# Quantised weights of two feed-forward layers: made in other stages, in pieces of 512 columns, and kept in DRAM as bf16

## The reference: what is computed

```python
def weight_quant(w):                     # w_gate, w_up, w_down: 2048*512 each
    scale = 1.0 / clip(mean(abs(w)), 1e-5)
    return clip(round(w * scale), -1.0, 1.0) / scale
```

```python
def absmean_quant(w):                    # w1, w2: 2048*512 each
    scale = mean(abs(w))
    mask = (abs(w) >= scale * 0.7)
    return sign(w) * mask
```

## Time and profile before

| | |
|---|---|
| median of three executions | 6014.61 us (6013.51 to 6016.92) |
| the profiled execution, its own time | 6023.15 us |
| span from its first to its last instruction | 6021.8 us |
| TensorE busy | 4680.2 us, 78% of the span |
| VectorE busy | 3349.2 us, 56% |
| POOL busy | 1794.8 us, 30% |
| ScalarE busy | 1542.7 us, 26% |
| mean granted clock of TensorE | 0.863 of full speed |

### The profile page before, as it was taken

One profiled execution on the slowest core, in us unless ns is written; L12 is line 12 of the kernel. 1 busy time (PEld: TensorE's weight loads), 2 busy tenths in 40 slices (PEclk: granted clock), 3 DMA queues, 4 the chain that ended last, 5 costly groups with the idle time before them and its releaser, 6 DMA issues. The chain is left out here.

```text
span 6021.8 us, 62767 instructions
## 1 busy us (share of the span) xinstructions
PE 4680.2 (78%) x22022; PEld 2480.6 (41%) x22022; DVE 3349.2 (56%) x5407; ACT 1542.7 (26%) x2993; POOL 1794.8 (30%) x1747
## 2 busy tenths in 40 slices
PE   6997888899965743278799889824999995996487
PEld 4664222344432632145333333322555552442276
DVE  4554777667749986899544445451333334355622
ACT  1111676411111100244222222201211210443132
POOL 0002222001126667134201111146555553011311
PEclk9997999999975556688899999957999997996598
DMA  2000000100000002200000000024999985001000
GB/s 74 1 1 8 2 1 2 67 0 0 0 9 0 1 0 28 92 15 1 20 1 13 7 1 8 1 93 113 229 239 233 218 193 148 1 1 67 2 1 28
DMA packets 127015, 288.74 MB, mean 48 GB/s; under 512 B 22113, under 2 KB 25825, under 8 KB 124258
## 3 DMA queue, kind: packets, MB, share of 16 engines
q1 hardware_dynamic: 79826, 184.42, 9.5%
q0 software_dynamic: 46880, 100.30, 8.5%
HBM read 345.47 MB, written 67.96 MB: 69 GB/s over the span
## 5 line engine op out<-in xcount | busy, mean ns | idle before, releaser
L204 PE MATMUL ps<-arena 128*128 128x512 f32 (+18 forms) x17578 | 4096.8, 473 | 709.9 <-DMA arena<-in_L_gamma 82.3
L204 PEld LDWEIGHTS ps<-arena 128*128 128x128 f32 (+6 forms) x17578 | 1918.5, 170 | 2674.8 <-issue 1446.3
L209 PE MATMUL ps<-arena 128*128 128x128 f32 (+2 forms) x3420 | 460.3, 278 | 579.6 <-DMA arena<-moe_x,arena 154.6
L209 PEld LDWEIGHTS ps<-arena 128*128 128x128 f32 (+2 forms) x3420 | 382.8, 144 | 764.2 <-issue 481.6
L253 POOL TENSOR_SCALAR arena<-arena 128x1 f32<-128x1 f32 x192 | 74.3, 387 | 1589.4 <-DVE arena L247 1589.1
L2559 DVE SCALAR_TENSOR_TENSOR arena<-ps,arena 128x128 f32<-128x128 f32 x382 | 103.7, 313 | 534.3 <-ACT arena L2443 534.3
L2618 POOL DMA_INDIRECT moe_y<-arena x191 | 306.5, 1605 | 301.8 <-DVE arena L2576 241.8
L2004 DVE TENSOR_REDUCE arena<-ps 128x2 f32<-128x256 f32 (+3 forms) x256 | 199.2, 821 | 332.5 <-PE ps L204 332.5
L800 DVE TENSOR_REDUCE arena<-ps 128x2 f32<-128x1024 f32 x256 | 304.0, 1219 | 82.6 <-PE ps L204 81.8
L774 ACT ACTIVATE arena<-ps 128x512 f32<-128x512 f32 x512 | 277.6, 597 | 126.6 <-PE ps L204 124.0
L1983 ACT ACTIVATE arena<-ps 128x1024 f32<-128x1024 f32 (+3 forms) x256 | 166.2, 701 | 542.1 <-PE ps L204 542.1
(11 more groups left out here) (299 smaller groups left out, 4180.6 us busy)
## 6 DMA issues: line engine op xcount, KB each, us to landing
arena<-in_L_ffn_gu SPq DMA_DIRECT2D x191, 768.0 KB
arena<-in_L_ffn_dn SPq DMA_DIRECT2D x191, 256.0 KB
arena<-in_L_ffn_dn SPq DMA_DIRECT2D x191, 128.0 KB, 3.7
moe_y<-arena SPq DMA_DIRECT2D x8, 1024.0 KB
arena<-moe_y SPq DMA_DIRECT2D x8, 1024.0 KB
arena<-in_L_ffn_w SPq DMA_DIRECT2D x8, 1024.0 KB
arena<-in_x SPq DMA_DIRECT2D x4, 1024.0 KB
arena<-in_L_attn_W_qkvu SPq DMA_DIRECT2D x4, 1024.0 KB
```

The lines of the kernel that those rows point to most:

```text
L204: return self.nc.tensor.matmul(out, lhsT, rhs, start=start, stop=stop, skip_group_check=True)
L209: return self.nc.tensor.transpose(out, in_, ident[0:n, 0:n])
```

## The change

The level one weights are no longer made in the mixing stage of level one but in the first attention, in 96 pieces of 512 columns (48 sums, 48 times three roundings), through three input buffers `bR` and two bf16 output buffers `bO`. Each finished piece is stored to an internal DRAM tensor `bD`, and the mixing stage of level one loads the three finished matrices of 2 MB straight into the places where they are used. The pieces are issued by one `advance` ahead of each step of the skewed order (two ahead of step 0), on TensorE and on VectorE; one piece on TensorE per matrix is the mean's matmul. SP issues all loads and stores after the stage's own loads.

The level three weights are made in level two's stream in the same manner (64 pieces: 32 sums, 32 pairs), at the steps t >= 4 with t % 4 != 2 (VectorE and TensorE from t = 10 on). SP walks over the stream's order too, so that its four reloads of weights now stand between ternary pieces. The mixing stage of level three loads the two finished matrices as bf16 into `TB`, and ScalarE copies them, 2048 columns at a time in front of every second exponential, into fp32r. The constants `k.bsc` move to the fixed part of SBUF, the memsets of the ones go along, and in `l1_xattn` the Hadamard matrix is loaded behind the inputs of the stage. What is computed stays the same.

```diff
+def bits_place(k):
+    k.bR, k.bO = [k.alloc([512]) for _ in range(3)], [k.alloc([512], BF16) for _ in range(2)]
+    k.bpart, k.bones = k.alloc([16]), k.alloc([P])
+    k.bD = k.nc.dram_tensor("bit_weights", [3, P, 8192], BF16, kind="Internal").ap()
+def bits_sp(k):
+    sp, dve, dma = k.sp, k.dve, k.dma
+    def leave(g):
+        n, c = divmod(g, 32)
+        if g >= 0 and c >= 16:
+            sp.wait_ge(dve, "bits", g)
+            dma.start(sp, k.bD[n, :, 512 * (c - 16):512 * (c - 16) + 512], k.bO[g % 2], "bits out", g)
+    for g in range(96):
+        n, c = divmod(g, 32)
+        w = rows(k.ins[BIT_WEIGHTS[n]])
+        c %= 16
+        sp.wait_ge(dve, "bits", g - 3)
+        dma.start(sp, k.bR[g % 3], w[:, c, :] if n == 2 else w[:, c // 4, c % 4 * 512:c % 4 * 512 + 512], "bits", g)
+        leave(g - 2)
+    leave(94)
+    leave(95)
 ...
+def bits_dve(k, ring):
+    nc, dve, dma = k.nc, k.dve, k.dma
+    for n in range(3):
+        for c in range(16):
+            g = 32 * n + c
+            dve.wait_ge(dma, "bits", g)
+            nc.vector.tensor_reduce(k.bpart[:, c:c + 1], k.bR[g % 3], AX.X, ALU.add, apply_absolute_value=True).then_inc(
+                *dve.done("bits", g))
+            yield
+        dve.settle()
+        nc.vector.tensor_reduce(k.bsc[:, n:n + 1], k.bpart, AX.X, ALU.add).then_inc(*dve.done("bsum", n))
+        yield
+        dve.wait_ge(k.pe, "bmean", n)
+        nc.vector.tensor_scalar(k.bsc[:, n:n + 1], ring.of("bmean", n)[:, 0:1], 1.0 / (2048 * 512), 1e-5, ALU.mult, ALU.max).then_inc(
+            *dve.done("bmean", n))
+        dve.wait_ge(dve, "bmean", n)
+        nc.vector.reciprocal(k.bsc[:, 4 + n:5 + n], k.bsc[:, n:n + 1]).then_inc(*dve.done("brec", n))
+        yield
+        dve.wait_ge(dve, "brec", n)
+        for c in range(16):
+            g = 32 * n + 16 + c
+            w, o = k.bR[g % 3], k.bO[g % 2]
+            dve.wait_ge(dma, "bits", g)
+            nc.vector.tensor_scalar(w, w, k.bsc[:, 4 + n:5 + n], 1.0, ALU.mult, ALU.min).then_inc(*dve.done("scaled", g))
+            dve.wait_ge(dve, "scaled", g)
+            nc.vector.tensor_scalar(w, w, -1.0, MAGIC, ALU.max, ALU.add).then_inc(*dve.done("rounded", g))
+            dve.wait_ge(dve, "rounded", g)
+            if c >= 2:
+                dve.wait_ge(dma, "bits out", g - 2)
+            nc.vector.tensor_scalar(o, w, MAGIC, None, ALU.subtract).then_inc(*dve.done("bits", g))
+            yield
 ...
+        bits_sp(k)
 ...
         part = k.thr_parts[0]
+        bits = bits_pe(k, R)
         for s, i in skew(NT, LAGS):
+            advance(bits, 1 if s else 2)
 ...
+        bits = bits_dve(k, R)
         for s, i in skew(NT, LAGS):
+            advance(bits, 1 if s else 2)
 ...
     def loads():
-        dma.start(sp, k.HM, ins["c_hadamard"], "hm")
         dma.start(sp, CT, ins["ctx_T"], "ct")
         dma.start(sp, W, ins["L1_xattn_W"], "w")
         dma.start(sp, gr[:, 0:1], ins["L1_gamma"], "gamma")
-        bits_loads(k)
+        dma.start(sp, k.HM, ins["c_hadamard"], "hm")
+        for n, w in enumerate((k.WG, k.WU, k.WD)):
+            dma.start(sp, w.rearrange("p a b -> p (a b)"), k.bD[n], "bits", n)
 ...
+def ternary_sp(k):
+    sp, dve, dma = k.sp, k.dve, k.dma
+    for g in range(66):
+        m = g - 2
+        if m >= 0 and m % 32 >= 16:
+            sp.wait_ge(dve, "tern", m)
+            dma.start(sp, k.tD[m // 32, :, 512 * (m % 16):512 * (m % 16) + 512], k.tO[m % 2], "tern out", m)
+        if g < 64:
+            n, c = g // 32, g % 16
+            w = rows(k.ins[TERNARY[n]])
+            sp.wait_ge(dve, "tern", g - 3)
+            dma.start(sp, k.tR[g % 3], w[:, c, :] if n else w[:, c // 4, c % 4 * 512:c % 4 * 512 + 512], "tern", g)
+        yield
 ...
+        for c in range(16):
+            g = 32 * n + 16 + c
+            dve.wait_ge(dma, "tern", g)
+            w, o = k.tR[g % 3], k.tO[g % 2]
+            if c >= 2:
+                dve.wait_ge(dma, "tern out", g - 2)
+            nc.vector.tensor_scalar(o, w, lo, None, ALU.is_le).then_inc(*dve.done("tlow", g))
+            dve.wait_ge(dve, "tlow", g)
+            nc.vector.scalar_tensor_tensor(out=o, in0=w, scalar=hi, in1=o, op0=ALU.is_ge, op1=ALU.subtract).then_inc(
+                *dve.done("tern", g))
+            yield
 ...
+            if t >= 4 and t % 4 != 2 and t < 140:
+                yield "ternary", t
 ...
+        part = ternary_sp(k)
+        for what, n in order():
+            if what == "ternary":
+                next(part, None)
+            elif (what, n) == ("q", 15):
+                sp.wait_ge(pe, "q", 15)
+                dma.start(sp, WQ, rows(ins["L2_xattn_q"]), "w_q", 1)
+            elif (what, n) == ("k", 15):
+                sp.wait_ge(pe, "k", 15)
+                dma.start(sp, WK[:, 0, :], ins["L2_xattn_k"], "w_k", 1)
+                for b in range(3):
+                    dma.start(sp, CT[b], ins["ctx_T"][:, b, :], "ct", b)
+            elif (what, n) == ("v", 15):
+                sp.wait_ge(pe, "v", 15)
+                dma.start(sp, WV[:, 0, :], ins["L2_xattn_v"], "w_v", 1)
+                dma.start(sp, CT[3], ins["ctx_T"][:, 3, :], "ct", 3)
+            elif (what, n) == ("out", 15):
+                sp.wait_ge(pe, "y", 15)
+                dma.start(sp, WO, rows(ins["L2_xattn_o"]), "w_o", 1)
 ...
-        ternary_loads(k)
+        for n in range(2):
+            dma.start(sp, TB[n], k.tD[n], "ternary", n)
 ...
+                if i % 2:
+                    n, c = divmod(i // 2, 4)
+                    w = (k.tW1, k.tW2)[n].rearrange("p a b -> p (a b)")
+                    act.wait_ge(dma, "ternary", n)
+                    nc.scalar.activation(w[:, 2048 * c:2048 * c + 2048], TB[n][:, 2048 * c:2048 * c + 2048], ACT.Copy).then_inc(
+                        *act.done("ternary"))
```

More of the change, by code:

```diff
@@ new lines, in bits_pe @@
+def bits_pe(k, ring):
+    for n in range(3):
+        for j in range(17):
+            yield
+        b = ring.take("bmean", n, by=((k.dve, "bmean", n),))
+        k.pe.wait_ge(k.dve, "bsum", n)
+        k.pe.wait_ge(k.pool, "bones")
+        k.mm(b[:, 0:1], k.bones, k.bsc[:, n:n + 1], True, True).then_inc(*k.pe.done("bmean", n))
+        for j in range(17):
+            yield
+def bits_dve(k, ring):
+    nc, dve, dma = k.nc, k.dve, k.dma
+    for n in range(3):
+        for c in range(16):
[26 more added lines that the diff above has]
+            yield
@@ L379, in l0_attn @@
     rs = k.alloc([NT, 4])
+    bits_place(k)
     similarity_parts(k)
+    assert k.off <= k.W - 5000
     k.ring = R
@@ L585, in gpsimd @@
     def gpsimd():
+        nc.gpsimd.memset(k.bones, 1.0).then_inc(*pool.done("bones"))
         for b in QT:
@@ L1388, in bit_weights @@
     k.WG, k.WU, k.WD = k.alloc([4, 2048], BF16), k.alloc([4, 2048], BF16), k.alloc([16, 512], BF16)
-    k.HM, k.bsc = k.alloc([P]), k.alloc([8])
+    k.HM = k.alloc([P])
     k.bitoff = k.off
[L1391 to L1402, removed]
@@ L1405, in bits_pe @@
[L1405 to L1436, removed]
-            nc.vector.tensor_scalar(w, w, k.bsc[:, 4 + n:5 + n], 1.0, ALU.mult, ALU.min).then_inc(*dve.done())
-            dve.settle()
-            nc.vector.tensor_scalar(w, w, -1.0, MAGIC, ALU.max, ALU.add).then_inc(*dve.done())
-            dve.settle()
-            nc.vector.tensor_scalar(W.rearrange("p a b -> p (a b)")[:, 2048 * j:2048 * j + 2048], w, MAGIC, None,
-                                    ALU.subtract).then_inc(*dve.done("bitw", n, j, 0))
-            yield
@@ L1553, in vector @@
                 k.norm(i)
-            elif what == "ticks":
-                advance(part, i)
     def gpsimd():
-        nc.gpsimd.memset(k.bones, 1.0).then_inc(*pool.done("ones"))
         for what, i in order():
@@ L1835, in loads @@
                 dma.start(sp, stg, ins["c_sel"], "sel")
[L1836 to L1846 removed]
+        part = ternary_sp(k)
[17 more added lines that the diff above has]
+                dma.start(sp, WO, rows(ins["L2_xattn_o"]), "w_o", 1)
     def tensor():
+        part = ternary_pe(k, R)
         for what, n in order():
             b, u = divmod(n, 16)
[L1851 removed]
+            if what == "ternary":
+                next(part, None) if n >= LOADED else None
+            elif what == "xt":
                 r = quad(R.take("xt", n, by=((act, "xt", n),)))
@@ L1989, in vector @@
         dve.wait_ge(pool, "ns0")
+        part = ternary_dve(k, R)
         for what, n in order():
             b, u = divmod(n, 16)
-            if what == "v" and n < NT:
+            if what == "ternary":
+                next(part, None) if n >= LOADED else None
+            elif what == "v" and n < NT:
                 b, t4 = divmod(n, 4)
@@ L2627, in l2_ffn @@
     gpsimd()
-def ternary_weights(k):
-    k.off = (k.off + 7) // 8 * 8
-    o = k.off
-    k.tF = [k.alloc([4, 2048]).rearrange("p a b -> p (a b)"), k.alloc([16, 512]).rearrange("p a b -> p (a b)")]
-    k.tW1, k.tW2 = k.rview(o, [4, 2048]), k.rview(o + 8192, [16, 512])
```

(13 more changed lines are left out.)

109 lines of the change are left out of this document (46 added, 63 removed).

## The result

The changed kernel takes 5953.52 us, median of three (5945.14 to 5955.56), against 6014.61: the ratio is 0.9894, with a 95% interval of 0.9872 to 0.9917. The forecast was 5941, in a range of 5905 to 5988. Its profiled execution took 5945.14 us (span 5943.8), 78 us less than the profiled one of before; the medians differ by 61.

A forecast was written before the change was run, and what follows sets the result against it. VectorE was taken to bound level one's mixing, a chain level three's, and TensorE the two stages taking work over. -63 - 45 + 30 + 4 = -74 us, from 6014.61 to 5941; range 5905 to 5988.

The forecast's parts named there:

- Level one, -63: Level one's mixing stage: VectorE's sums and roundings go, last mix ends near 2499 instead of 2562; -63 us, bounds -75 to -54.
- two holes: Level one's mixing stage: 1.5 us left open in each of two blocks, where learned tiles may not hide behind mixes.
- Level three, -45: Level three's mixing stage: ternary work leaves the chain, a pass falls from 10.9 to 7.3 us; -45 us, between -50 and -34.
- Rival (c): Level three's chain keeps much of its length through copies and keys, giving 20 us and not 45: 5966 us; chance 0.12.
- The first attention, +30: First attention: 104 us of VectorE work arrives, not all covered by idle time; +30 us, between +5 and +76.
- Six triple passes: First attention: two triple pieces between L577 and L551 overflow a slack of 0.86 us in six passes; 14 us.
- The two pieces ahead of L577 go into its wait: First attention: two pieces ahead of L577 are covered by VectorE's wait there for POOL, 2.3 us on average.
- Rival (a): First attention hides all but 5 us of the added work: -99 us, 5916 us; chance 0.2.
- Rival (b): First attention: TensorE's clock gives way in 14 passes, 46 us besides the 30: -28 us, 5987 us; chance 0.13.
- (d): First attention: stores landing later than 4.7 us hold VectorE before 48 triples; at 9 us landing, 6147 us; chance 0.03.
- (e): First attention: work only changes its stage, TensorE waits out all 104 us: 6015 us; chance 0.02.
- Level two's stream, +4: Level two's stream: 62 us of added VectorE pieces mostly fall into its waits for TensorE; +4 us, between 0 and +20.

The follow-up runs named there:

- none between: Changed kernel with four input and four output buffers and no level one piece between L577 and L551 in the first attention: 5920.8 us, ratio 0.9844.
- one piece more: Changed kernel with one level one piece more between L577 and L551 and one less ahead of step 0: 5963.2 us, ratio 0.9911.
- five ahead of v: Changed kernel with four input and four output buffers, five of a pass's seven pieces ahead of v's copy, two ahead of the first step: 5912.8 us, ratio 0.9830.

## Why the prediction was right, and where it was off

- **The time.** 5953.5 against 5941: 12.5 above, and well inside the range. By profiled executions it was 5945 against 5949. The sum of the four stages was -75.1 against -74. That this came so near is in part luck: level one gave 5.0 us more than forecast and the first attention took 5.0 more. The gain is 61 us by the medians, and 66 in another batch for almost the same code with more buffers.
- **Level one, -63, measured -68.0.** Taken apart: the first mix came 1.3 us sooner than walked through, of the 3 us for two holes 2.2 weren't there, and the last mix of before ended 1.5 us later than the 2562 used. The largest term that was mis-sized is thus the two holes: the later blocks still had steps of 1.70 us, and they hid. The 1.3 us lie in the second block's tiles, at 1.15 us and not the 1.70 of the earlier trace rows. That does not need the VectorE work to be gone: the kernel with the level three half alone keeps all of it, and its second block comes at 1.15 too, with a mean clock of 0.61 over the stage:

```profile
2437.79 0.58 ACT L1516 ACTIVATE arena<-ps 128x512 f32<-128x512 f32 x1
...
2438.94 0.58 ACT L1516 ACTIVATE arena<-ps 128x512 f32<-128x512 f32 x1
```

- **Level three, -45, measured -45.5.** The pass of 7.3 us came out at 7.33. The copies were charged 1 us; the doubled copies (+0.5) speak for a charge of that size. Rival (c) falls.
- **The first attention, +30, measured +35.0.** Six triple passes were put at 14 us: 2.95, 4.66, 4.66, 2.17, 2.14 and 3.51, 20.1. Sum passes: 1.2 for 3. Filling: 2.3 for 7. The means: 5.3 for 4. The clock: 6.1 for 2. The total hides a wrong step. "The two pieces ahead of L577 go into its wait" failed: one of them stands ahead of the norm with which POOL's chain starts, so it moves L577 and the wait's end alike. The stage's length moved with the pieces between about as priced, in the kernels with none and with one more, though half of that was busy time and not waits. And they were not all: taking out those alone left 9.6 us, and only the kernel with five ahead of v got to 2.8. That kernel moves both pieces ahead of L577. The one that moves the norm's piece alone cut the waits for the decayed queries from 19.4 to 11.0 but not the stage, so how much that one piece cost is not shown.
- **Rival (a)**, that the stage could hide all but 5 us, was wrong for this order; another order of the same work gets to 2.8, with 3.2 us of it given back by TensorE's busy time.
- **Rival (b)**, the clock, with 46 us, falls: TensorE's busy time grew by 6.1, and its clock stayed at 0.94. The pair of rows that it rested on (12.60 behind a wait of 0.78, 15.93 behind one of 2.11) says less than was read into it: the kernel before has such a group of 88 at 15.86 us behind a wait of 0.78 too, and the changed one has 14.23 behind 2.11. Something of the mechanism is there in small: in the changed kernel the group of 24 records takes 10.54 us behind four waits of 0.58 to 2.17 and 11.96 to 13.49 behind six of 2.11 to 5.21, and the kernel with one piece more paid 14.8. The Trainium skill, TensorE: Matmul & The Clock Gate, A second HAM failure mode, says that brief, frequent idles between groups can make the clock swing; the rows of 24 agree with it, with 6 to 15 us as its size here.
- **Rivals (d) and (e)** fall: VectorE waits for no store, and of some 104 us TensorE waited out 28.9. The Trainium skill's rule in DMA: Bandwidth & Descriptors, Anatomy of one DMA, gives about 2 us and the bytes for its GpSimd path, by which a 256 KB load would take an estimated 2.6 us; those of SP's queue in the kernel with none between land in 3.3 to 3.7. The prediction used that figure for stores that SP issues, and their landing is not in the rows.
- **Level two's stream, +4, measured +3.4.** No run took this apart; with the level three half alone the stream took 950.6 us.

## What to carry to other kernels

In an in-order queue a piece of moved work is hidden only by an idle stretch that lies behind it and ahead of the next result that somebody wants. Here 245 us of idle VectorE said little, and the one wait ahead of v said most. Before you put work "into a wait", ask where the awaited engine's own work starts: if it starts behind your piece, the wait moves with it. Place filler right ahead of the engine's longest wait for the bounding engine, and double or quadruple a suspected cost to find the room it has. When a test gives the length that was expected, see whether it also gives the waits.

## What was not expected of the hardware

- TensorE's mean granted clock in level one's mixing rose from 0.63 to 0.74 as VectorE's work left it, but the stretch at the upper level did not grow: worked out from these means and the stage's length it is some 38 us before and 37 after, an estimate. What went is time at the lower level. A tile's step in the second block took 1.70 us before and 1.15 in the kernel with the level three half alone, whose code is the same there; what decides that is open.
- One and the same first attention took 573.2, 572.7, 566.7 and 566.6 us in four kernels. They are the changed one, the level one half alone, and the ones with two and with four copies. With two copies TensorE's waits for L638 are 25.6 us instead of 30.7 and its busy time is the same (465.6): a few waits fall to either side of the slack.
- Level two's experts, untouched, took 1198 to 1204 us in eleven profiled executions, and 1214 and 1218 in the two of one batch, in which the kernel before had a median 11 us above that of the result. The cause is open.
